# Moving some fifty entries of a hand-written step schedule in a decoder layer with three attention stages and a mixture of experts

## Chip, cores and metric
One core of a Trainium2 chip (trn2) runs the whole program in one launch. The metric is the device time of that core in microseconds (us). TensorE is called PE here, VectorE DVE, ScalarE ACT, GpSimd POOL, and SyncE, which issues nearly all DMAs, SP.

## The reference, cut to what matters
Sixteen sequences of 128 tokens with 256 channels go through three sublayers, each followed by a plain layernorm.

```
x = layernorm(x + attn(x))                 # stage A: 16 heads of 16, rope, causal
x = layernorm(x + xattn(x, mask, ctx))     # stage B: 32 heads of 8, rope, mask; and 32 adapter heads over ctx
x = layernorm(x + ffn(x))                  # ffn: stage C, 16 heads of 128; stage D, 4 experts, top 2
def attn(x):   q, k, v = split(x @ Wqkv.T + b); q, k = rope(q), rope(k)
               return softmax(q @ k.T * scale + causal) @ v @ Wo.T + bo
```

## The kernel before
**Steps and units.** Stages A and B are one long software pipeline over numbered steps, from -20 up. Each engine's program is a Python loop over the same step numbers: at every step it looks in dictionaries for what is due and emits it, so each engine has its work in an order fixed at build time. Engines meet at semaphores alone. A *unit* is four heads of one sequence. Stage A has 64 units, one in a step (steps 0 to 63), four for a sequence; stage B has 256 units, two in every even step from 64 on, sixteen for a sequence (eight of self-keys, with the mask, and eight of adapter keys).

**One unit.** `pass1` computes the scores with queries down the partitions (L541 or L547 put the mask in, L554 the products), and DVE takes the negated row maxima (L737). Once a sequence has all its maxima, `shift_parts` splits them into three bf16 parts (L450 to L456, four small operations, on DVE in A and on POOL in B), PE turns them (`shift`, L565) and SP writes them as rows into the stacked queries. `pass2`, 12 steps later in A and 28 in B, computes the scores with keys down the partitions, already shifted (L589); ACT takes the exponential (L985), in stage B after DVE has added the mask (`mask2` L746, then L978). `pv`, two steps later, multiplies by the values (L611). Maxima of unit n free the score bank of unit n + 2, so `pass1` is never more than two units ahead of DVE.

**Outputs of a sequence g.** `ends`: ACT copies the result out of its bank (L995, L997). `tos`: PE turns it (L621), and DVE divides in the next step (L757 to L777). `backs`: PE turns it back (L631), and ACT and DVE split it in the next step (L1007, `out_low` L788 and L791). `wos`: PE's output projection (six matmuls L472 to L474), and in the next step DVE's `residual` (L801, then the three layernorm statistics L695, L697, L699). Two steps after that POOL computes the power, and DVE's `finish` (L710; POOL in B) writes X at three.

**Inputs of a pair of sequences c.** `xts`: four transposes of x or of the context (L489), which ACT and DVE split at the next step (`x_high` L888, `x_low` L723). In the steps up to 64 DVE does `x_low` before its maxima. `projs`: projections of q and k (12 matmuls on PE; from pair 9 on in two halves, one step apart), from which `evacs` (ACT L907, L909), `ropes`, `sums`, `splits` (POOL and a few on DVE: L403, L416, L427, L437, L440; ACT L926, L929), `parts` (DMA out) and `stacked` (DMAs into the stack, three for a sequence and kind in A, six in B) follow at fixed distances. `vals`: value projections (six matmuls). `masked`, `clamps`: the mask. POOL clears and fills the value buffers of stage B at the steps of `INITS` (`init_values`, L1075), and ACT's `values` waits for that.

**Banks.** The small products of PE (transposes, projections, values, shifts, outputs) take three PSUM banks in turn, two from step 86 on. The table `home` gives the banks out in the order in which the dictionaries name the products, so a product waits until the one three (or two) before it in this order has been read.

**Within a step** PE does pass1, pass2, pv, then the small products in the order `xts`, second halves, `projs`, `masked`, `vals`, turns (`turned`, `tos`, `backs`), `wos`; from step `TURNED_FIRST` on the turns come first. DVE does `x_low`, maxima, the outputs (divide, `out_low`, residual), `shift_parts`, mask, rope, splits, clamp, finish; in the steps of `CHANGE` the outputs come before the maxima.

**The way into stage C.** From step 302 on the same loops also do the loads of stage C's first weights (`LOAD_W`, `LOAD_W2`, `LOAD_TABS`), the first layernorm (`NORMS`), the splits (`HIGHS` on ACT L1736, `LOWS` L1645, `X_LOW` L1507) and the first four projections (`PROJECTIONS`, six matmuls of 512 columns, L1518 to L1520) with their ropes (`ROPES`, DVE L1658, L1661, POOL L1822). Stages C and D have schedules of their own.

## Time and profile before

| | us |
|---|---|
| median of 3 runs (1191.92 to 1195.79) | 1195.52 |
| the profiled execution | 1195.52 |
| its span, first to last instruction | 1193.7 |
| stages A and B with their start-up, to the last unit's maxima | 527.2 |
| stages C and D, from 575 us | 618.7 |
| PE busy over the span | 1128.8 |
| DVE busy over the span | 993.6 |
| mean granted clock of PE | 0.990 |

The profiled execution took 1.8 us more than its span and lies on the median, so sums are made against 1195.5. Busy PE is not PE at its peak, as ends of matmuls are modelled; what counts in the schedule is where an engine sits idle, and for whom.

### The profile page before, as it was taken

What the parts mean: (1) busy time and instruction counts of PE and PEld (TensorE: products, weight loads), DVE (VectorE), ACT (ScalarE), POOL (GpSimd) and SP (SyncE); (2) the same over time, 40 slices, a digit from 0 to 9 for tenths busy, and PEclk for the clock granted to TensorE, in tenths of its full rate; (3) what the DMA queues carried; (4) which work ended last, traced back from release to release, by engine and by line L of the source; (5) the groups of instructions that cost most, each with busy time, mean ns of one, the idle gap of its engine ahead of it and who ended that gap; (6) DMA issues with size and microseconds to landing.
All of it is one profiled execution on the core that took longest, in us unless ns stands there. A gap on an engine that the chain in (4) does not pass through costs nothing.

```text
span 1193.7 us, 29551 instructions
## 1 busy us (share of the span) xinstructions
PE 1128.8 (95%) x11172; PEld 934.4 (78%) x11172; DVE 993.6 (83%) x2284; ACT 660.4 (55%) x1687; POOL 656.9 (55%) x706
## 2 busy tenths in 40 slices
PE   5899999899999999879999999999999999999997
PEld 5667666666776766546899899998999899997887
DVE  6768887888889898978888888888888888877977
ACT  5466554566766667565555444444444444558663
POOL 4467655545455455254778544544554454847665
PEclk9899999999999999999999999999999999999999
DMA  6875443334333433212222000000000100101111
GB/s 161 205 186 135 122 125 87 87 95 116 88 106 101 106 97 97 76 58 76 68 63 63 1 1 2 1 1 2 1 1 1 37 1 1 37 18 37 36 36 36
DMA packets 98670, 76.68 MB, mean 64 GB/s; under 512 B 73547, under 2 KB 86987, under 8 KB 98529
## 3 DMA queue, kind: packets, MB, share of 16 engines
q1 hardware_dynamic: 98529, 74.80, 23.1%
q8 instruction: 89, 1.46, 0.5%
q14 instruction: 52, 0.43, 0.1%
HBM read 53.86 MB, written 19.92 MB: 62 GB/s over the span
## 4 chain that ended last, share of the span: by engine, by line
PE 58%; DVE 23%; issue 7%; ACT 5%; POOL 3%; SPq 2%; DMA 2%; DVEq 0%; POOLq 0%; ACTq 0%
PE bank L1518 5%; DVE B_nr L737 4%; PE bank L1519 4%; PE bank L1520 4%; PE bank L1574 4%; PE bank L1547 4%; PE bank L611 4%; DVE PT L746 3%; PE bank L472 2%; PE bank L554 2%; SPq L1154 2%; PE bank L1534 2%; PE bank L1589 2%; PE bank L1587 2%; PE bank L1588 2%
## 5 line engine op out<-in xcount | busy, mean ns | idle before, releaser
L1822 POOL TENSOR_TENSOR C_QK<-C_t1b,C_t2b 128x512 f32<-128x512 f32 x128 | 168.9, 1320 | 226.6 <-DVE C_t2b L1661 226.0
L1658 DVE SCALAR_TENSOR_TENSOR C_t1b<-bank,C_bcol,C_tabs 64x512 f32<-64x512 f32 x256 | 192.0, 750 | 37.3 <-PE bank L1520 33.2
L737 DVE TENSOR_REDUCE B_nr<-bank 128x4 f32<-128x512 f32 x256 | 164.4, 684 | 22.6 <-PE bank L554 21.0
L1518 PE MATMUL bank<-C_XTh,C_Wh 128*128 128x512 f32 x256 | 111.9, 437 | 4.4 <-DVE C_t2b L1661 1.9
L985 ACT ACTIVATE PT<-bank 128x512 f32<-128x512 f32 x160 | 92.2, 598 | 39.8 <-PE bank L589 39.3
L1754 ACT ACTIVATE C_P<-bank,C_nm 128x128 f32<-128x128 f32 x256 | 90.7, 367 | 34.0 <-DVE C_nm L1671 32.4
L978 ACT ACTIVATE PT<-PT 128x512 f32<-128x512 f32 x96 | 59.3, 630 | 88.7 <-DVE PT L746 88.7
L1773 ACT ACTIVATE C_V<-bank 128x512 f32<-128x512 f32 x64 | 38.1, 597 | 124.1 <-PE bank L1536 122.5
L611 PE MATMUL bank<-PT,vpool 128*32 128x128 f32 x2048 | 97.4, 285 | 4.3 <-ACT PT L978 3.1
L1519 PE MATMUL bank<-C_XTl,C_Wh 128*128 128x512 f32 x256 | 101.2, 395 | 0.0
L1520 PE MATMUL bank<-C_XTh,C_Wl 128*128 128x512 f32 x256 | 100.8, 394 | 0.0
L1661 DVE SCALAR_TENSOR_TENSOR C_t2b<-bank,C_bcol,C_tabs 128x512 f32<-128x512 f32 x128 | 96.1, 751 | 1.8
L554 PEld LDWEIGHTS bank<-stk 48*128 48x128 bf16 (+1 forms) x1280 | 50.9, 96 | 52.3 <-issue 27.5
L554 PE MATMUL bank<-stk 48*128 48x128 bf16 (+1 forms) x1280 | 77.7, 221 | 9.6 <-DVE B_nr L737 8.9
L589 PE MATMUL bank<-stk 54*128 54x128 bf16 (+1 forms) x1280 | 76.5, 219 | 10.0 <-DVE PT L746 3.8
L1762 ACT ACTIVATE C_OTh<-bank,C_bcol 128x512 fp32r<-128x512 f32 x64 | 44.1, 690 | 73.6 <-PE bank L1574 73.0
L1682 DVE SCALAR_TENSOR_TENSOR C_OTl<-bank,C_bcol,C_OTh 128x512 fp32r<-128x512 f32 x64 | 47.9, 748 | 38.9 <-ACT C_OTh L1762 38.8
L705 POOL TENSOR_TENSOR rstd<-ve,mhalf 128x1 f32<-128x1 f32 x48 | 28.1, 584 | 91.1 <-DVE ve L699 91.1
L589 PEld LDWEIGHTS bank<-stk 54*128 54x128 bf16 (+1 forms) x1280 | 53.5, 95 | 27.8 <-DVE PT L746 6.8
L1534 PE MATMUL bank<-C_Wh,C_XTh 128*128 128x256 f32 x256 | 72.5, 283 | 1.6 <-DVE C_t2b L1661 1.3
L1587 PE MATMUL bank<-C_Wh,C_OTh 128*128 128x256 f32 x256 | 72.0, 281 | 0.4 <-DVE C_OTl L1682 0.4
L1535 PE MATMUL bank<-C_Wl,C_XTh 128*128 128x256 f32 x256 | 71.9, 281 | 0.0
(267 smaller groups left out, 3683.5 us busy)
## 6 DMA issues: line engine op xcount, KB each, us to landing
Adrq<-PB SPq DMA_DIRECT2D x16, 192.0 KB, 3.2
Adrk<-PB SPq DMA_DIRECT2D x16, 192.0 KB, 3.4
stk<-Adrq SPq DMA_DIRECT2D x16, 192.0 KB
stk<-Adrk SPq DMA_DIRECT2D x16, 192.0 KB
Bdrq<-PB SPq DMA_DIRECT2D x16, 192.0 KB, 2.7
stk<-Bdrq SPq DMA_DIRECT2D x32, 96.0 KB
Bdrk<-PB SPq DMA_DIRECT2D x16, 192.0 KB, 2.7
stk<-Bdrk SPq DMA_DIRECT2D x32, 96.0 KB
```

What stands on the lines that cost most here:

```text
L554: m = e.matmul(bank[n % 2][:, j * 128:j * 128 + 128], QS[L][i3][rows, h, :], (AS if kd else KS[L])[i3][rows, h, :], start=bool(kd), stop=b ...
L589: m = e.matmul(bank2(n)[:, j * 128:j * 128 + 128], (AS if kd else KS[L])[i3][rows, h, :], QS[L][i3][rows, h, :], start=bool(L), stop=bool( ...
L611: m = e.matmul(o[32 * j:32 * j + 32, c3 * 128:c3 * 128 + 128], vp[:, h, :], pt_of(n)[:, j * 128:j * 128 + 128], start=first or not L, stop ...
L737: e.tensor_reduce(dst, bank[n % 2][:, :].rearrange("p (a b) -> p a b", a=4), AX.X, ALU.max, negate=True).then_inc(sem("m_dve"), 1)
L1518: e.matmul(o[:, :], CWh[hp][:, cs], XCh[0][:, t, :], start=t == 0, stop=False)
L1519: e.matmul(o[:, :], CWh[hp][:, cs], XCl[0][:, t, :], start=False, stop=False)
L1520: m = e.matmul(o[:, :], CWl[hp][:, cs], XCh[0][:, t, :], start=False, stop=t == 1)
L1534: e.matmul(ob, XCh[0][:, t, xs], CWh[hp][:, cs], start=t == 0, stop=False)
L1587: e.matmul(o, OCh[:, bs], CWh[hp][:, cs], start=r == 0 and b % 2 == 0, stop=False, skip_group_check=True)
L1658: e.scalar_tensor_tensor(out=v4(t1b[kq][lo:lo + 64, :]), in0=v4(o[hi:hi + 64, :]), scalar=bc[hi:hi + 64, :], in1=tabsC[hi:hi + 64, 2 * kq ...
L1661: e.scalar_tensor_tensor(out=v4(t2b[kq][:, :]), in0=v4(o[:, :]), scalar=bc, in1=tabsC[:, 2 * kq, :].unsqueeze(1).to_broadcast([128, 4, 128 ...
L1822: e.tensor_tensor(QK[v % 3][:, kq, :], t1b[kq][:, :], t2b[kq][:, :], ALU.add).then_inc(sem("rc_pool"), 1)
```

## The change
Only numbers of the schedule change: no operation is added, removed or reshaped, and the same instructions run on the same engines in another order. `s` is the step number.

```diff
-    LOAD_B, SPLIT_B = (14, 20, 27, 26), (20, 27)
+    LOAD_B, SPLIT_B = (12, 20, 24, 28), (20, 27)
...
-    xts = places((-1,), (-2, -4), (-2, 4), (-8, 8))
-    projs = places((2, 6), (2, 6, 10), (0, 10, 13), (-4, 10, 13))
-    masked = places((), (11,), (23,), (18,))
-    clamps = {s - (6 if c < 10 else 7): c for s, (c, _) in masked.items()}
-    vals = places((3, 5), (0, 14, 8, 16), (19, 22, 20, 25), (6, 22, 26, 30))
+    xts = places((-1,), (-2, -4), (-2, 2), (-8, 8))
+    projs = places((2, 6), (2, 6, 10), (0, 8, 13), (-5, 10, 13))
+    masked = places((), (12,), (21,), (18,))
+    clamps = {s - (3 if c < 10 else 7): c for s, (c, _) in masked.items()}
+    vals = places((3, 5), (4, 15, 8, 16), (19, 22, 20, 24), (7, 23, 26, 30))
...
-        xts[bg0(c_) - (4 if c_ < 2 else 7)] = (c_, 0)
+        xts[bg0(c_) - (4 if c_ == 1 else 4 if c_ == 2 else 4)] = (c_, 0)
...
-        for b_, late in enumerate((0, (8, 7, 13)[ti_]) if c_ > 8 else (0, 0)):
+        for b_, late in enumerate((0, (7, 7, 13)[ti_]) if c_ > 8 else (0, 0)):
...
-        return end_step(g, kd) + (7 if 17 <= g < 31 and kd else 1)
+        return end_step(g, kd) + (7 if 16 <= g < 31 and kd else 1)
...
-        return to_step(g, 1) + (6 if g < 14 else 6 if g < 15 else 5 if g < 17 else 8 if g < 31 else 5)
+        return to_step(g, 1) + (4 if g < 14 else 4 if g < 15 else 8 if g < 16 else 8 if g < 31 else 5)
...
-    backs = {wo_step(g) - (2 if g == 14 else 4 if g == 15 else 3 if 16 <= g < 31 else 2): g for g in range(32)}
+    backs = {wo_step(g) - (2 if g == 14 else 3 if g == 15 else 3 if 16 <= g < 31 else 2): g for g in range(32)}
-    turned = {shift_step(g) + (2 if g < 17 else 4 if g < 31 else 2): g for g in range(32)}
+    turned = {shift_step(g) + (2 if g < 16 else 4 if g < 31 else 2): g for g in range(32)}
...
-    LOAD_W, LOAD_W2, LOAD_TABS, TURN, X_LOW, VALUES, LOAD_PAIR2 = 305, 330, 315, 319, 324, 352, 352
-    NORMS = [303, 304, 306, 307, 310, 312, 313, 314]
+    LOAD_W, LOAD_W2, LOAD_TABS, TURN, X_LOW, VALUES, LOAD_PAIR2 = 302, 332, 317, 319, 321, 352, 352
+    NORMS = [303, 305, 307, 309, 311, 312, 313, 314]
-    HIGHS, LOWS = [308, 310, 342, 351], [322, 323, 351, 352]
-    PROJECTIONS = {(0, 0): 326, (0, 1): 335, (1, 0): 341, (1, 1): 344}
-    ROPES = {(0, 0): 328, (0, 1): 339, (1, 0): 342, (1, 1): 345}
+    HIGHS, LOWS = [308, 310, 337, 351], [322, 323, 351, 352]
+    PROJECTIONS = {(0, 0): 327, (0, 1): 335, (1, 0): 341, (1, 1): 343}
+    ROPES = {(0, 0): 328, (0, 1): 338, (1, 0): 342, (1, 1): 344}
-    MASK_FIRST = 316
+    MASK_FIRST = 320
...
-    CHANGE = range(70, 82)
-    TURNED_FIRST = 87
+    CHANGE = range(66, 84)
+    TURNED_FIRST = 82
...
-    INITS = {28: (0, 0), 35: (0, 1), 53: (1, 0), 61: (1, 1), 67: (2, 0), 73: (2, 1), 80: (3, 0), 89: (3, 1)}
+    INITS = {31: (0, 0), 35: (0, 1), 55: (1, 0), 59: (1, 1), 63: (2, 0), 71: (2, 1), 79: (3, 0), 88: (3, 1)}
```

Written out, the main moves are these:

| what | step before | step after |
|---|---|---|
| stage A, x of pairs 2 to 7 turned (`xts`) | 8c - 27 | 8c - 24 |
| stage A, turned back, sequences 0 to 14 | 4g + 23 | 4g + 21 |
| stage A, output projection, sequences 0 to 14 | 4g + 25 | 4g + 23 |
| the same two, sequence 15 | 80, 84 | 84, 87 |
| POOL's filling of the fourth value buffer | 61 | 59 |
| first and second values of pair 8 on the self side | 44, 58 | 48, 59 |
| pair 9: context turned, keys projected, last stacks | 68, 74, 87 and 94 | 66, 72, 85 and 92 |
| sequence 16: to, back, output projection | 110, 112, 115 | 116, 121, 124 |
| stage B, q projection of pairs 10 to 15, halves | r = 28, 29 | r = 27, 28 |
| the second q stack of these pairs | r = 49 | r = 47 |
| the first two values of these pairs | r = 6, 22 | r = 7, 23 |
| stage C's last early projection | 344 | 343 |

Here r is the step less 64, modulo 32 (a pair of sequences of stage B takes 32 steps; 49 and 47 are those of the next period).

## Rows read from the trace of the kernel before

**Rows 1.** The page's first part: busy time of PE and DVE over the span.

```profile
PE 1128.8 (95%) x11172; PEld 934.4 (78%) x11172; DVE 993.6 (83%) x2284; ACT 660.4 (55%) x1687; POOL 656.9 (55%) x706
```

**Rows 2.** Windows, stretches: length, busy PE, PEld, DVE, ACT, POOL, PEclk, DMA, GB/s.

```profile
0.00:57.20 57.20, 40.78 (x311) 33.99 (x311) 40.80 (x68) 27.99 (x59) 28.56 (x36) 0.94 0.73 182
...
99.90:118.70 18.80, 18.80 (x208) 13.94 (x206) 16.00 (x36) 11.54 (x28) 13.53 (x20) 1.00 0.51 119
...
177.20:222.70 45.50, 41.88 (x451) 30.04 (x451) 36.23 (x88) 22.13 (x64) 25.23 (x46) 0.99 0.32 87
...
401.20:444.30 43.10, 41.76 (x652) 30.09 (x646) 38.52 (x76) 29.51 (x77) 22.45 (x30) 1.00 0.38 101
```

**Rows 3.** Timeline of DVE, steps 36 to 39 of stage A: start, length, instruction [idle before].

```profile
109.26 0.69 DVE L737 TENSOR_REDUCE A_nr<-bank 128x4 f32<-128x512 f32 x1 [1.14 <-PE bank L554]
...
110.49 0.60 DVE L788 SCALAR_TENSOR_TENSOR OTl<-bank,A_bcol,OTh 128x128 fp32r<-128x128 f32 x2
111.00 1.02 DVE L450 CAST A_nmb<-A_nr 128x16 bf16<-128x16 f32 x1
112.06 0.65 DVE L452 TENSOR_TENSOR A_nb<-A_nr,A_nmb 128x16 f32<-128x16 f32 x1
...
114.13 0.41 DVE L710 TENSOR_SCALAR X<-z,mv,rstd 128x256 f32<-128x256 f32 x1
114.45 1.28 DVE L737 TENSOR_REDUCE A_nr<-bank 128x4 f32<-128x512 f32 x2
...
116.85 0.68 DVE L737 TENSOR_REDUCE A_nr<-bank 128x4 f32<-128x512 f32 x1
```

**Rows 4.** Timeline of POOL in the same steps.

```profile
110.82 1.17 POOL L440 TENSOR_TENSOR PB<-y,PB 128x512 bf16<-128x512 f32 x1 [0.27 <-ACT PB L929]
111.95 1.42 POOL L416 TENSOR_TENSOR tt<-ab,vpool 128x256 f32<-128x256 f32 x2
```

**Rows 5.** Timeline of PE and DVE, step 34, with a projection of pair 6.

```profile
104.70 0.39 PE L472 MATMUL bank<-XTh,A_Wh 128*128 128x256 f32 x1
...
106.49 0.39 PE L541 MATMUL bank<-identb,causalTb 128*128 128x512 bf16 x1
...
105.04 1.28 DVE L737 TENSOR_REDUCE A_nr<-bank 128x4 f32<-128x512 f32 x2
```

**Rows 6.** Timeline of DVE and POOL, step 30: the residual beside a POOL operation.

```profile
97.00 0.43 DVE L695 BATCH_NORM_STATS2 stat<-z 128x6 f32<-128x256 f32 x1
...
96.72 1.16 POOL L437 TENSOR_TENSOR y<-y,PB 128x512 f32<-128x512 f32 x1 [0.74 <-ACT PB L926]
```

**Rows 7.** Timeline of PE: its waits at steps 16, 30, 62 and 92.

```profile
60.12 0.40 PE L589 MATMUL bank<-stk 99*128 99x128 bf16 x4 [2.85 <-DMA stk<-A_nmT]
...
96.18 0.22 PE L565 MATMUL bank<-identb,A_nmb 128*48 128x128 bf16 x1 [0.53 <-DVE XTl L723]
...
172.54 0.43 PE L611 MATMUL bank<-PT,vpool 128*32 128x128 f32 x8 [1.05 <-ACT OTf L995]
...
222.11 0.61 PE L554 MATMUL bank<-stk 48*128 48x128 bf16 x8 [1.45 <-DVE B_nr L737]
```

**Rows 8.** Timeline of PE and DVE in one period of stage B, steps 218 to 224.

```profile
394.26 0.40 PE L554 MATMUL bank<-stk 48*128 48x128 bf16 x8
...
394.03 0.41 DVE L791 TENSOR_TENSOR OTl<-bank,OTh 128x256 fp32r<-128x256 f32 x1
394.67 1.29 DVE L737 TENSOR_REDUCE B_nr<-bank 128x4 f32<-128x512 f32 x2 [0.23 <-PE bank L554]
...
401.19 1.29 DVE L737 TENSOR_REDUCE B_nr<-bank 128x4 f32<-128x512 f32 x2 [0.40 <-PE bank L554]
```

**Rows 9.** Timeline of PE, steps 344 and 348, on the way into stage C.

```profile
553.61 0.40 PE L589 MATMUL bank<-stk 54*128 54x128 bf16 x8
...
554.89 0.50 PE L1518 MATMUL bank<-C_XTh,C_Wh 128*128 128x512 f32 x1 [0.31 <-DVE C_t2b L1661]
...
559.26 0.39 PE L472 MATMUL bank<-B_Wh,OTh 128*128 128x256 f32 x1 [0.56 <-DVE OTl L791]
```

## The prediction
> **What bounds the kernel now.** I read the page's first part first, then the windows, then the timelines engine by engine. PE is busy for 1128.8 of 1193.7 us and DVE for 993.6 [rows 1]. The windows show where what is left lies. The start, to 57.2 us, holds 16.4 us of idle PE (57.20 - 40.78). In steps 32 to 39 of stage A PE is busy for all of 18.80 us and DVE for 16.00; a period of stage B takes 43.1 us with 41.76 of PE and 38.52 of DVE [rows 2]. So PE sets the pace in A and B, with DVE 10 to 15% behind, and the two are coupled tightly: maxima free score banks, and pass1 is at most two units ahead of them. No operation changes, so all that can change is PE's idle time, and an order can hurt as easily as help: in A some 15% of slack on DVE stands against PE's none.
>
> The start is bound elsewhere. PE waits 2.85 us at step 16 for a DMA of shift rows [rows 7]. That DMA stands behind SP's queue of stack DMAs, whose places the change doesn't move before it. What is gained before 60.1 us is therefore taken back at this wait, and stages C and D keep their own schedules.
>
> **Stage A, DVE.** Four steps make one group. DVE's run that matters starts with maxima(4k) and ends with maxima(4k+1), since pass1(4k+3) waits for the latter. Before, it holds divide, out_low (0.60), the four small operations, rope and finish (0.41), and lasts 5.8 us: from 109.26 to the first end in the row of 114.45 [rows 3]. The change puts the output projection two steps earlier, so out_low and finish leave the run for step 4k+2 and the residual enters it. Its four operations are all that DVE does from the end of the two maxima, 115.7, to the next at 116.85, so some 1.2 us [rows 3]. Taken plainly that is 1.2 - 0.6 - 0.4 = +0.2 us for the run.
>
> But the small operations aren't limited by themselves. L450 lasts 1.02 us and ends at 112.02, and POOL's L440 ends at 111.99; L452 takes 0.65 and ends with the first half of POOL's L416 [rows 3, 4]. They sit waiting for POOL. A start 0.6 us later (1.2 - 0.6) only shortens that wait, as 1.02 us of L450 has 0.8 us of it to give, and the run loses finish: -0.4 us. The residual's own operations keep their length beside POOL: L695 takes 0.43 us under a POOL operation of 1.16 [rows 6]. I take -0.4, and +0.6 (a run that gets longer by all that moves in ahead of the small operations, with finish's place not regained) stays as the upper end. The Trainium skill has the mechanism (SBUF — State Buffer, section "SBUF: two separate sides"): DVE and GpSimd lock a shared port pair, and the loser blocks for the whole instruction. By that rule the result is this -0.4; were the lengths the operations' own, it would be +0.2.
>
> PE's part of a group: the output projection (six matmuls, 0.70 us: L472 to L474 at 0.117 each) moves from step 4k+1 to 4k+3 and the turn back (0.22) the other way. That is -0.48 before pass1(4k+3) and +0.48 behind it. Where DVE's run ends first this sums to nothing; with the run at -0.4 it does so in nearly every group. Term: 0, upper end below.
>
> **Stage A, the x transposes.** In 8c - 24 a transpose stands at step 4k, and its x_low is the first thing DVE does in step 4k+1, right behind the long run. Giving out the banks in the new order, I find that the projection of step 4k+2 takes the bank of this transpose: step 26 behind that of pair 6, step 34 behind that of pair 7. At step 34 PE would start at 104.70; DVE's run ends at 105.04, less 0.4, plus x_low 0.68 is 105.3 [rows 5]. So PE waits 0.65 us there, and as much at step 26: +1.3. Against that goes the old conflict, 0.53 us at step 30, which waited for x_low of pair 7 [rows 7]: -0.5. Pair 5's transposes (0.41 us) move from step 13, where the wait at 60.1 covered them, to step 16: +0.4. At steps 40 to 43 both have the same two waits for x_low.
>
> **Other places up to step 96.** At step 62 PE waits 1.05 us for ACT's copy of the result; ACT stood in `values`, waiting for POOL to fill the value buffer at step 61 [rows 7]. It is filled at 59 now: -1.05. At step 92 PE waits 1.45 us for maxima, with nothing else due [rows 7]; the first half of pair 10's q projection (0.70 us) now fills this: -0.7. The moves of sequence 15, of pair 9 and of g = 16 shift work inside a stretch with 3.6 us of idle PE (45.50 - 41.88) [rows 2]: 0, and 1.5 either way. `MASK_FIRST` changes nothing: the only output projection from 316 to 319 is at 316, and its residual's step 317 has no mask operation.
>
> **Stage B, six periods.** Before, steps 220 and 221 hold 18 matmuls (both halves of the q projection and the output projection) beneath 3.8 us of DVE work. The first half goes to step 219. PE's pass1(220), at 394.26, then starts 0.7 later, and DVE, free at 394.44, waits 0.93 instead of 0.23 [rows 8]. DVE gets 0.40 back at 401.19, where it waited for PE [rows 8]: +0.3 is left. The splits of q come one step earlier on POOL, so that POOL's sum of the two results can be earlier in step 230, where PE and DVE are both a little idle; that may give the 0.3 back. I take +0.1 a period, six times: +0.6. The bounds are -0.3 (all of that comes, and no delay) and +0.7 (nothing is absorbed): -1.8 and +4.2.
>
> **Way into C.** The last early projection (six matmuls of 512 columns, 1.4 us) goes ahead of pass2 at 344. It waits for L1661, before and after, and can't start ahead of 554.89; the 1.28 us of pass2 and pv from 553.61 to 554.89, which covered the wait, now come behind it: +1.28 [rows 9]. Later PE waits 0.56 for out_low at 559.26, which absorbs as much [rows 9]: +0.7 is left. HIGHS at 337 puts 1.06 us of ACT where exponentials are due, X_LOW goes ahead of LOWS on POOL, the norms lie in odd steps: +0.1 together, bounds -1 and +1.
>
> **Sum.** 1.3 - 0.5 + 0.4 - 1.05 - 0.7 + 0.6 + 0.7 + 0.1 = +0.85 us: 1195.5 + 0.8 = 1196.3.
>
> **Rivals.** 0.3% is 3.6 us, about what a measurement of this kernel can tell from no change.
>
> *No measurable change* is the forecast, 0.42.
>
> *Slower, DVE's run in A.* Place: step 4k, where the residual now stands ahead of the small operations. If these move away from POOL's operations instead of ending with them, or POOL is late too, the run grows by 0.6 instead of shrinking by 0.4. Seven of the groups of steps 24 to 60 then have DVE last (those without an x transpose or a moved value projection): 7 x 0.6 = 4.2, and both x_low waits grow by 1.0: +2.0. With the 0.8 of the sum this makes +7.0: 1202.5. It passes 0.3% from about 0.1 us a group on, with the two waits. For it: DVE's slack in A is only 15% [rows 2], and even at step 34, where PE has work to spare, pass1(35) at 106.49 comes 0.8 us after the first maxima of the row of 105.04 [rows 5]. Against: L450's length [rows 3, 4]. Chance 0.16.
>
> *Slower, stage B.* The 0.7 us isn't absorbed: +4.2 instead of +0.6, 1199.9. For it: between its waits at 394.67 and 401.19 DVE has 6.1 us of work on end [rows 8]. Against: 0.40 of idle DVE right behind. Chance 0.14.
>
> *Faster.* The new order spreads PE's small products: in stage B 6, 12 and 12 matmuls where 6 and 18 stood, in A none beside the long run. With the waits of 0.53, 1.05 and 1.45 gone (-3.0), x_low in time (0), stage B at -1.8 and the way into C even, it is about -4.8: 1190.7. For it: 3.6 us of idle PE from 177 to 223 and 1.3 in each period [rows 2]; against: each such gap is behind one particular operation. [...] Chance 0.28.
>
> **How the numbers follow.** Predicted is the likeliest case, 1196.3. With it, its own range is 1192 to 1199. The range takes in the faster case to 1190 and most of the slower ones to 1203. Faster 0.28, same 0.42, slower 0.30 (0.16 + 0.14).
>
> **What would show it.** In the profile after: PE waiting about 0.65 us for L723 at the projections of steps 26 and 34; no waits of 0.53 at step 30 and 1.05 at step 62; L450 shorter than 1 us in A, and L454 still ending with L416; step 16's wait at about 60 us still there; the periods of stage B at 43.1 to 43.4 us; L589 of the pair 316 behind the projection. The prediction is wrong if a period of B changes by more than 0.5, if the 120 us from step 16 to 64 change by more than 3, or if a stretch of half granted clock comes or goes with a new or a lost wait (the windows show 0.94 in the start [rows 2]).

## The result, and the profile after

| | before | after |
|---|---|---|
| median, us | 1194.85 (1191.92 to 1195.79, 6 runs) | 1205.91 (1202.71 to 1207.78, 6 runs) |
| the profiled execution, its span | 1195.52, 1193.7 | 1203.91, 1202.1 |
| granted clock over the span | 0.990 | 0.988 |

The ratio is 1.0094 (95% interval 1.0079 to 1.0109): the change costs 11 us, 0.94%. The forecast was 1196.3, and its range ended at 1203.

The page's first part answers to [rows 1]: PE is busy for 4.0 us more, DVE for 3.6 less, with the same instructions. No work came in; what was lost is order, and in this profile a little clock.

```profile
PE 1132.8 (94%) x11172; PEld 934.2 (78%) x11172; DVE 990.0 (82%) x2284; ACT 659.2 (55%) x1687; POOL 654.7 (54%) x706
```

**A trap ahead.** The two profiles can't be laid side by side as they are. At the first maxima of step 64 the kernel before stands at 177.16 and the one after at 176.88, which looks like a stage A that cost nothing. But the profiled execution of before had a stretch of half granted clock at 61.7 us, right behind the wait of step 16, and the one after had none there. The experiment with the new way into C alone (below, `tail_alone`) has the order of the kernel before up to step 302 and a clock like that after: both show two stretches of half clock ahead of step 16 and none from there to step 64. So it is the ruler for everything ahead of step 318. "Ruler" below always means this run. Windows, columns as in [rows 2]: first the kernel before from step 16 to 20, then `tail_alone`, cut at the first maxima of steps 16, 20, 64, 152, 284 and 318.

```profile
57.16:71.42 14.26, 11.41 (x114) 7.81 (x114) 5.11 (x10) 7.88 (x16) 5.91 (x7) 0.88 0.74 200
```

```profile
57.42:68.64 11.22, 9.90 (x114) 6.88 (x114) 5.11 (x10) 8.03 (x17) 6.19 (x7) 1.00 0.90 229
68.64:174.33 105.69, 102.14 (x1109) 74.74 (x1108) 89.36 (x196) 64.80 (x161) 69.26 (x101) 1.00 0.54 136
174.33:301.00 126.67, 119.84 (x1643) 85.23 (x1645) 105.73 (x219) 76.24 (x199) 65.12 (x99) 0.99 0.37 97
301.00:477.31 176.31, 170.28 (x2656) 122.88 (x2646) 157.03 (x307) 120.67 (x313) 90.49 (x117) 1.00 0.37 99
477.31:522.15 44.84, 37.72 (x645) 24.32 (x639) 41.78 (x89) 25.32 (x54) 12.99 (x19) 1.00 0.29 81
```

The kernel after, cut at the same maxima:

```profile
56.76:69.03 12.27, 10.39 (x118) 7.34 (x118) 5.72 (x11) 8.72 (x18) 6.26 (x7) 1.00 0.72 185
69.03:176.88 107.85, 103.42 (x1115) 75.33 (x1114) 88.36 (x200) 64.11 (x161) 67.67 (x100) 1.00 0.55 136
176.88:304.20 127.32, 118.94 (x1638) 83.42 (x1641) 104.76 (x217) 76.00 (x199) 66.01 (x100) 1.00 0.36 96
304.20:484.62 180.42, 171.83 (x2656) 122.60 (x2644) 157.06 (x306) 120.64 (x312) 90.50 (x117) 1.00 0.36 97
484.62:530.00 45.38, 37.78 (x645) 24.37 (x639) 41.79 (x90) 25.34 (x54) 12.98 (x19) 1.00 0.29 81
```

The same order takes 14.26 us with a clock of 0.88 and 11.22 with 1.00. Not all of these 3.04 us is the clock: PE's busy time differs by 1.51 (11.41 against 9.90), and the rest is the wait of step 16 for its DMA, 2.85 us before and 1.32 in the ruler. In the eleven kernels that have the order of before up to this wait it took from 0.44 to 2.85 us. Without it steps 16 to 20 take 9.90 or 9.91 us in the five of them with full clock there.

Against the ruler the change costs 1.05 us in steps 16 to 20, 2.16 to step 64, 0.65 to step 152, 4.11 to step 284 and 0.54 to step 318; 0.66 us of it had been won before step 16 (57.42 - 56.76). That is 7.85 us; the way into C brings the rest. Of the 1.05 us, 0.56 is a longer DMA wait (1.88 against 1.32) and 0.49 the order (10.39 against 9.90). The ruler's third window holds a stretch of half clock that the kernel after doesn't have, so the 0.65 us there are too few; against `q_half_alone`, which has none either, they are 1.23.

**Stage A.** PE's waits after (timeline of PE; the last is on the way into C):

```profile
58.75 0.40 PE L589 MATMUL bank<-stk 99*128 99x128 bf16 x4 [1.88 <-DMA stk<-A_nmT]
83.43 0.39 PE L472 MATMUL bank<-XTh,A_Wh 128*128 128x256 f32 x1 [0.72 <-DVE XTl L723]
103.97 0.39 PE L472 MATMUL bank<-XTh,A_Wh 128*128 128x256 f32 x1 [0.72 <-DVE XTl L723]
220.16 0.38 PE L472 MATMUL bank<-B_Wh,XTh 128*128 128x256 f32 x1 [1.12 <-DVE z L801]
555.98 0.64 PE L611 MATMUL bank<-PT,vpool 128*32 128x128 f32 x8 [0.71 <-ACT PT L978]
```

The waits for x_low at steps 26 and 34 are there, at 0.72 each (forecast 0.65); those of 0.53 and 1.05 of [rows 7] are gone. The wait at 220.16 is new. DVE and POOL at step 36, timelines, answer to [rows 3, 4]:

```profile
109.05 0.69 DVE L737 TENSOR_REDUCE A_nr<-bank 128x4 f32<-128x512 f32 x1 [0.80 <-PE bank L554]
...
111.49 0.32 DVE L450 CAST A_nmb<-A_nr 128x16 bf16<-128x16 f32 x1
...
112.52 0.66 DVE L454 CAST A_nmb<-A_nb 128x16 bf16<-128x16 f32 x1
...
113.90 1.29 DVE L737 TENSOR_REDUCE A_nr<-bank 128x4 f32<-128x512 f32 x2
```

```profile
110.61 1.16 POOL L440 TENSOR_TENSOR PB<-y,PB 128x512 bf16<-128x512 f32 x1 [2.10 <-ACT PB L929]
111.73 1.42 POOL L416 TENSOR_TENSOR tt<-ab,vpool 128x256 f32<-128x256 f32 x2
```

L450 shrank from 1.02 to 0.32 us and still ends with L440 (111.81 and 111.77); L454 ends with L416 (113.18 and 113.15). From the first maxima to the next it is 4.85 us (113.90 - 109.05) where it was 5.19 (114.45 - 109.26): the run of DVE got 0.34 shorter, and -0.4 was forecast. Here the trace agrees with the rule of the Trainium skill that the prediction cited (SBUF — State Buffer, section "SBUF: two separate sides").

**Stage B.** Steps 218 to 224 after, timelines of PE and DVE; they answer to [rows 8]:

```profile
396.36 0.39 PE L472 MATMUL bank<-XTh,B_Wh 128*128 128x256 f32 x1 [0.37 <-DVE OTl L791]
...
397.27 0.40 PE L554 MATMUL bank<-stk 48*128 48x128 bf16 x8
```

```profile
395.89 0.42 DVE L791 TENSOR_TENSOR OTl<-bank,OTh 128x256 fp32r<-128x256 f32 x1
397.71 1.29 DVE L737 TENSOR_REDUCE B_nr<-bank 128x4 f32<-128x512 f32 x2 [1.40 <-PE bank L554]
...
404.17 1.29 DVE L737 TENSOR_REDUCE B_nr<-bank 128x4 f32<-128x512 f32 x2 [0.36 <-PE bank L554]
```

The half projection (396.36) waits for out_low, which holds the bank that it takes, and out_low stands behind the maxima on DVE. Then come its six matmuls, then pass1, then DVE, which has been idle for 1.40 us instead of 0.23.

And the 0.40 us at 401.19, which was to give part of it back, is still 0.36. PE was on its way to give it back: it starts pass1 of step 222 at 400.02, 1.32 us ahead of DVE's maxima (401.34), where it had been 0.59 ahead. But then its value product waits for ACT's copy out of the projection's bank (L907). This copy stands on ACT behind an exponential (L978) that waits for DVE's mask operation, which follows the late maxima. Timelines of PE and ACT after:

```profile
401.83 0.39 PE L472 MATMUL bank<-B_Wh,XTh 128*128 128x256 f32 x1 [0.50 <-ACT ab L907]
```

```profile
399.62 1.23 ACT L978 ACTIVATE PT<-PT 128x512 f32<-128x512 f32 x2 [2.96 <-DVE PT L746]
...
401.13 0.65 ACT L907 ACTIVATE ab<-bank 128x256 f32<-128x256 f32 x2
```

All four profiles with pairs 12 to 15's half at the new step have this wait of 0.50 us in each of the four periods, and none of the other fourteen has it. (This is read from the traces; no run takes this wait away alone.)

DVE's idle 1.40 us stands at steps 156, 188 and 252 too. The maxima come 1.17 us later at each of the four places, and 0.15 comes back within the period.

### The profile page after: what moved, and what is told of

The parts are those of the page before. It is cut to its first block, busy times and chain, and to the rows that moved or that the text cites. A ratio compares the mean times of both kernels' runs of the same rounds, so it can differ in the third digit from the quotient of the medians.

```text
span 1202.1 us, 29553 instructions
## 1 busy us (share of the span) xinstructions
PE 1132.8 (94%) x11172; PEld 934.2 (78%) x11172; DVE 990.0 (82%) x2284; ACT 659.2 (55%) x1687; POOL 654.7 (54%) x706
## 3 DMA queue, kind: packets, MB, share of 16 engines
q8 instruction: 89, 1.46, 0.5%
## 4 chain that ended last, share of the span: by engine, by line
PE 61%; DVE 23%; issue 7%; ACT 5%; DMA 2%; POOL 2%; SPq 1%; DVEq 0%; POOLq 0%; ACTq 0%
PE bank L1518 5%; PE bank L1519 5%; PE bank L1520 4%; PE bank L1574 4%; PE bank L611 4%; PE bank L1547 4%; DVE B_nr L737 3%; PE bank L547 3%; DVE PT L746 3%; PE bank L472 3%; PE bank L554 2%; PE bank L589 2%; PE bank L1534 2%; PE bank L1589 2%; PE bank L1587 2%
## 5 line engine op out<-in xcount | busy, mean ns | idle before, releaser
L737 DVE TENSOR_REDUCE B_nr<-bank 128x4 f32<-128x512 f32 x256 | 164.5, 685 | 27.0 <-PE bank L554 25.9
L978 ACT ACTIVATE PT<-PT 128x512 f32<-128x512 f32 x96 | 59.4, 630 | 91.6 <-DVE PT L746 91.6
L440 POOL TENSOR_TENSOR PB<-y,PB 128x512 bf16<-128x512 f32 x36 | 42.2, 1171 | 54.9 <-ACT PB L929 54.6
```

The source lines that it names most:

```text
L737: e.tensor_reduce(dst, bank[n % 2][:, :].rearrange("p (a b) -> p a b", a=4), AX.X, ALU.max, negate=True).then_inc(sem("m_dve"), 1)
```

## The experiments

Each was timed in five rounds beside the kernel before; a ratio is to that kernel, with its 95% interval. 1% is 12 us. "Maxima" are the starts of L737 in the profile, against `tail_alone`, the ruler.

### The q projection's half, and who waits for whom

`q_half_alone`, on the kernel before:

```diff
-    projs = places((2, 6), (2, 6, 10), (0, 10, 13), (-4, 10, 13))
+    projs = places((2, 6), (2, 6, 10), (0, 10, 13), (-5, 10, 13))
```

> The kernel before with one number changed: the first half of stage B's q projection at r = 27 (-5 where it has -4). Theory 1: 1.17 us in each of the four periods from step 156 on and about as much in the two before, 5 to 7 us slower: 1200 to 1202 us. Theory 2: 0.6 us slower, 1195.5 us, and the periods stay at 43.1 us. A third possibility is that the half costs its full price only together with the values' move from r = 6 to 7: then this kernel shows 0.70 a period, 4.2 us, with no wait for out_low.

1198.25 us, ratio 1.0049 (1.0032 to 1.0065): this one number is half of the loss. The timeline of DVE at step 220:

```profile
394.29 1.29 DVE L737 TENSOR_REDUCE B_nr<-bank 128x4 f32<-128x512 f32 x2 [1.39 <-PE bank L554]
```

PE's half projection waits 0.38 us for out_low there, without the values' move, so the third possibility falls. From step 152 to 284 the maxima lose 4.13 us, four times 1.03. Pairs 10 and 11 lose nothing, against theory 1: no out_low stands ahead of their halves.

`q_half_back`, the changed kernel:

```diff
-    projs = places((2, 6), (2, 6, 10), (0, 8, 13), (-5, 10, 13))
+    projs = places((2, 6), (2, 6, 10), (0, 8, 13), (-4, 10, 13))
```

> The changed kernel with one number back: the first half of stage B's q projection at step r = 28 again (-4 where the change has -5). Theory 1: the half stands between maxima n and pass1 n + 2, in a loop of PE and DVE that has no slack: its six matmuls (0.70 us) and a wait of 0.37 us for out_low, whose bank it takes, push DVE's next maxima back by 1.17 us and nothing is given back later. Four periods show exactly 1.17 us, the two before them something near it: the kernel gets 4.7 to 7 us faster, 1199 to 1201 us, and DVE's idle 1.40 us in front of the maxima of steps 156, 188, 220 and 252 goes back to 0.2. Theory 2, the prediction's term: the half costs 0.1 us a period and the 1.17 us have another cause (the order of the banks, the values one step later): 0.6 us faster, 1205.3 us, and the idle time stays.

1200.01 us, ratio 1.0054 (1.0038 to 1.0070): 0.40% less than the change (1.0094 - 1.0054), 4.8 us. DVE's idle time at step 220 is 0.24 again. Theory 1's price holds from both sides; its split into wait and matmuls does not, as the next run shows.

`back_early`, the changed kernel with the turn back a step earlier:

```diff
-    backs = {wo_step(g) - (... else 3 if 16 <= g < 31 else 2): g for g in range(32)}
+    backs = {wo_step(g) - (... else 4 if 16 <= g < 31 else 2): g for g in range(32)}
```

> The changed kernel with the turns back of stage B's sequences one step earlier (four steps ahead of the output projection instead of three), so that out_low stands behind the maxima one unit earlier and the q projection's first half finds its bank read. Theory: of the 1.17 us a period that the half costs, 0.37 us is the wait for out_low and goes; the 0.70 to 0.8 us of matmuls stay: four periods, 1.5 us faster than the changed kernel, and the idle time of DVE before the maxima of steps 156, 188, 220 and 252 goes from 1.40 to 1.0 us. Rival: out_low, 0.42 us, ahead of the maxima of the unit before takes the place of the wait: no gain, and a wait of PE for maxima instead. A third: the bank rule makes something else late, and it is slower.

1200.70 us, ratio 1.0052 (1.0037 to 1.0066), 5.0 us less than the change where 1.5 had been expected (in the profiles it is 3.1 between steps 152 and 284). DVE at steps 154 and 156:

```profile
306.15 0.42 DVE L791 TENSOR_TENSOR OTl<-bank,OTh 128x256 fp32r<-128x256 f32 x1
...
309.51 1.29 DVE L737 TENSOR_REDUCE B_nr<-bank 128x4 f32<-128x512 f32 x2 [0.87 <-PE bank L554]
```

out_low now stands ahead of the maxima (307.36), and the half doesn't wait. A period costs 0.26 us instead of 1.03 (the maxima stand 3.89 us behind `tail_alone`'s at step 152 and 4.91 at step 284, four periods later). My split of the 1.17 us into 0.37 of wait and 0.70 of matmuls was wrong. Without the wait most of the 0.70 us lies beside the maxima on DVE, for which pass1 waits anyway; with it, the whole half starts only when DVE has done the maxima and out_low, and nothing hides it. The bank's wait was worth some 0.8 us a period.

`b_back_only` is the control: the same diff on the kernel before.

> The kernel before with the turns back of stage B's sequences one step earlier (four steps ahead of the output projection) and the q projection's halves where they were. In the changed kernel this move was worth 0.8 us a period. Theory: it was worth that because the first half waited for out_low's bank; with the half at r = 28 nobody waits for it at r = 27, and the move gives nothing or costs a little, as out_low (0.42 us) now stands ahead of the maxima of r = 26: 0 to +0.3 us in each period, 0 to 1.5 us slower. Rival: the move helps by itself, 0.8 us in each of four or five periods: 3 to 4 us faster, 1190 us, and the best version.

1196.99 us, ratio 1.0028 (1.0015 to 1.0042). The move alone gains nothing: it costs 0.24 us a period, and 1.7 us about step 112, where sequence 16's turn back moves. So it was worth its 0.8 us only for the half.

### The way into stage C, and the clock

`tail_alone`: the new LOAD_*, X_LOW, NORMS, HIGHS, PROJECTIONS and ROPES on the kernel before; `tail_back`: the old ones on the changed kernel.

> The kernel before with the change's numbers for the way into stage C alone (loads, NORMS, HIGHS, LOWS, X_LOW, PROJECTIONS, ROPES). In the two profiles this stretch cost 3.9 us more after the change. Theory 1: some 2.7 us of it are a stretch of half granted clock that went on for 10.2 us where 3.4 had been, which hangs on the moment at which the chip looks and not on this order; the order itself costs 0.7 us (exponentials behind the split of HIGHS) and 0.4 us (the last projection ahead of pass2): 1.0 us slower in the median, 1195.9 us. Theory 2: the order causes the longer stretch of half clock: 3 to 4 us slower, 1198 to 1199 us, with 0.60 or less of granted clock in the profile's windows from 530 to 540 us.

> The changed kernel with the numbers of the way into stage C as before. Theory 1 (the long stretch of half clock isn't this order's doing): 1.0 us faster than the changed kernel, 1204.9 us. Theory 2 (it is): 3 to 4 us faster, 1202 to 1203 us, and the stretch of half clock near 540 us is 3.4 us long.

1194.84 us, ratio 1.0013 (1.0003 to 1.0023), and 1202.88 us, ratio 1.0085 (1.0071 to 1.0098), 0.09% less than the change: 1.1 to 1.6 us, theory 1. The 1.1 us of `tail_back` lie inside the intervals (the change's starts at 1.0079); the 1.6 us of `tail_alone` are clear of the kernel before (its interval starts at 1.0003). Yet the clock in the profiles went with the order. Windows of 20 us from the last maxima on, of before, after, `tail_alone` and `tail_back`:

```profile
528.00:548.00 20.00, 16.57 (x260) 9.97 (x260) 13.23 (x28) 15.27 (x29) 11.94 (x12) 0.91 0.21 70
```

```profile
532.00:552.00 20.00, 17.01 (x212) 10.27 (x212) 12.23 (x24) 13.04 (x25) 11.10 (x13) 0.74 0.12 35
```

```profile
524.00:544.00 20.00, 16.85 (x212) 10.32 (x212) 12.19 (x25) 12.96 (x25) 11.07 (x13) 0.74 0.13 33
```

```profile
535.00:555.00 20.00, 16.83 (x264) 10.00 (x266) 13.29 (x28) 15.29 (x29) 11.77 (x12) 0.91 0.23 70
```

Both with the new order have 0.74, both with the old one 0.91. But `back_early`, with the new order, had one short stretch of half clock there (3.4 us), and `q_half_alone`, with the old one, a longer one (6.8 us). Over all profiles, a stretch of 10.2 us came in two of the four with the new order and in none of the fourteen with the old one, where the longest was 6.8. Whether the order makes the long stretch likelier stays open; the medians bound what it costs.

### Stage A

`x_alone`, on the kernel before:

```diff
-        xts[bg0(c_) - (4 if c_ < 2 else 7)] = (c_, 0)
+        xts[bg0(c_) - (4 if c_ < 2 else 4)] = (c_, 0)
```

> The kernel before with the x transposes of pairs 2 to 7 at 8c - 24 instead of 8c - 27, and nothing else. The prediction's own steps give two new waits of 0.65 us for x_low at steps 26 and 34, and the old wait of 0.53 at step 30 gone: +0.8 us, 0.07% slower. Between kernels with the same clock history the profiles of the old and the new order of stage A differ by 2.2 us from step 20 to step 64. Theory 1: the transposes cost more than their waits, as 0.66 us of them and x_low ahead of the maxima now stand in steps 4k and 4k + 1, where PE or DVE has nothing to spare: 1.8 to 2.5 us from step 20 to 64, 0.2% slower. Theory 2: the outputs' move carries the rest: 0.8 us here. In times alone the two are within the uncertainty; the maxima's starts in the profile tell them apart.

1195.56 us, ratio 1.0014 (1.0005 to 1.0023). From step 20 to 64 the maxima lose 0.39 us, nearer to the prediction's 0.8 than to theory 1. Its steps 16 to 20 had a stretch of half clock at 59.6 us. Less the DMA wait they take 11.91 us, and 11.41 in `out_alone`, which has the old order there and a like stretch at 59.9: pair 5's transposes cost 0.5 us, where +0.4 was forecast. The kernel after shows the same price at full clock (10.39 against 9.90).

`out_alone`, on the kernel before:

```diff
-        return to_step(g, 1) + (6 if g < 14 else 6 if g < 15 else 5 if g < 17 else 8 if g < 31 else 5)
+        return to_step(g, 1) + (4 if g < 14 else 4 if g < 15 else 5 if g < 17 else 8 if g < 31 else 5)
```

> The kernel before with the output projections of sequences 0 to 14, and the turns back two steps ahead of them, two steps earlier, and nothing else. The prediction has 0 for it (PE's -0.48 and +0.48 cancel, DVE's run is 0.4 us shorter), and as a rival +0.6 us in each of seven groups, 4.2 us. Theory 1: the run is shorter (L450 goes from 1.02 to 0.32 us), but PE, with the projection's 0.70 us now behind pass1 of 4k + 3, delays the maxima of 4k + 4 by 0.7 us where the run gives back 0.3 to 0.5: +0.1 to +0.2 us a group, +1.3 us from step 20 to 64, 0.1% slower. Rival 1: the prediction's 0 holds, and the profile shows less than 0.3 us from step 20 to 64. Rival 2: +4.2 us, 0.35% slower.

1197.65 us, ratio 1.0033 (1.0020 to 1.0046), 3.9 us, and 2.9 us of maxima from step 20 to 60 (2.0 at steps 61 and 62, where DVE has given its share back). The prediction had 0. The view of PE's waits from 70 to 168 us (waiting operation, releaser, sum, times, longest):

```profile
PE bank L565 <- DVE XTl L723: 0.9, 2, 0.6
PE bank L621 <- DVE XTl L723: 0.9, 1, 0.9
PE bank L472 <- ACT ab L909: 0.8, 1, 0.8
PE bank L489 <- DVE XTl L723: 0.7, 1, 0.7
PE bank L621 <- DVE OTl L788: 0.6, 1, 0.6
PE bank L541 <- DVE A_nr L737: 0.3, 2, 0.2
```

They sum to 4.2 us; in `tail_alone` from 68.6 to 164 us they sum to 2.5 (0.9, 0.6, 0.5, 0.3, 0.2), and none is for L737 or L788. Some 1.7 us more are thus waits, most of them of small products for a bank. The rest is seen at steps 38 to 40, the timeline of PE in `out_alone`:

```profile
115.41 0.39 PE L541 MATMUL bank<-identb,causalTb 128*128 128x512 bf16 x1 [0.16 <-DVE A_nr L737]
...
118.95 0.39 PE L541 MATMUL bank<-identb,causalTb 128*128 128x512 bf16 x1
```

At 115.41 PE is early, since the output projection has left, and waits for maxima: what it saved isn't collected. At 118.95 the projection's 0.70 us stand in front, and maxima(40) come 0.78 us later against `tail_alone`, of which the shorter run gives 0.34 back. (From step 60 to 64 this profile loses 2.0 us more, beside a stretch of half clock at 175.9 us, so the timed 3.9 us are not all the order's.)

`a_back_only`, on the kernel before:

```diff
-    backs = {wo_step(g) - (2 if g == 14 ...
+    backs = {wo_step(g) - (4 if g < 14 else 2 if g == 14 ...
```

> The kernel before with the turns back of stage A's sequences 0 to 13 two steps earlier (step 4g + 21), their output projections left at 4g + 25. Stage A's outputs moved together cost 2.9 us from step 20 to 60 in the profile. Theory: that price is the output projection's, whose 0.70 us now stands ahead of pass1 of 4k + 4 and is missed by nobody ahead of pass1 of 4k + 3, which waits for maxima; the turn back is 0.22 us and out_low leaves a run that ends with POOL anyway: less than 0.5 us either way from step 20 to 60, no change in the times (within 0.1%). Rival: the turns back and out_low carry the price or a gain of their own: 0.2 us a group, 2 us.

1202.16 us, ratio 1.0073 (1.0055 to 1.0091). Theory and rival are both far off: a move of 0.22 us of matmuls costs 8.7 us. PE's waits from 73 to 176 us:

```profile
PE bank L472 <- DVE XTl L723: 3.3, 2, 1.8
PE bank L565 <- DVE OTl L788: 2.6, 3, 1.6
```

Both are new. With the turn back two steps earlier, `home` gives the shift (L565) a bank that out_low still has to read, and PE, which works in its order, stands still. The larger sum is two projections, at steps 30 and 41, that now wait for x_low (1.51 and 1.80 us). Two stretches of half clock inside stage A (at 128.7 and 156.0 us) came with it in the profile, so the 8.7 us are waits and clock together.

### The stretch from step 60 to 128

`init_g16`: the new INITS, and sequence 16 at the places of the later ones (`to_step` + 7, `wo_step` + 8, `turned` + 4), on the kernel before.

> The kernel before with two parts of the change that the profiles show as gains: the filling of the value buffers at the new steps (INITS, the fourth at step 59) and sequence 16's output at the places that the later sequences have (to_step + 7, then 8, turned + 4). Theory: the wait of 1.0 us at step 62 goes, and about 0.5 us around steps 112 to 128: 1.0 to 1.5 us faster than before, 0.1%, and the best version of all so far. Rival: each gain is given back at the next wait behind it (the maxima of step 64, the q stack of step 126): no change.

1194.11 us, ratio 0.9996 (0.9988 to 1.0005): the rival. Timeline of PE at step 64:

```profile
173.48 0.50 PE L547 MATMUL bank<-B_MKh,B_identr 128*128 128x512 f32 x1 [0.82 <-DMA stk<-Bdrk]
```

The wait of 1.0 us at step 62 is gone, and the first unit of stage B waits 0.82 us for its keys' DMA instead. Sequence 16 gives 0.9 us from step 110 to 130, but the maxima of step 96 come 2.0 us later; what that is, the last two runs tell.

`three_back`: the changed kernel with the half, stage A's outputs and the way into C as before.

> The changed kernel with three of its parts as before: the q projection's first half at r = 28, stage A's output projections and turns back at their old steps, and the numbers of the way into stage C. Theory: the prices are additive, and of the 0.94% that the change costs these three carry 0.40 + 0.33 + 0.09 to 0.13%: 0.1% above the kernel before is left, 1195.5 us. Rival: a part that was taken at nothing (the stretch from step 64 to 128, the values, the loads) costs on its own: 0.3% or more above before.

1196.30 us, ratio 1.0035 (1.0021 to 1.0048): the rival. 4.2 us are left, and the maxima lose 2.0 of them from step 64 to 128. So I looked at sequence 15, whose residual was waited for at 220.16.

`seq15_alone`, on the kernel before (projection at 87 instead of 84, turn back at 84 instead of 80):

```diff
-        return to_step(g, 1) + (... 5 if g < 17 ...)
+        return to_step(g, 1) + (... 8 if g < 16 else 5 if g < 17 ...)
-    backs = {wo_step(g) - (... 4 if g == 15 ...
+    backs = {wo_step(g) - (... 3 if g == 15 ...
```

> The kernel before with sequence 15's output projection at step 87 instead of 84 and its turn back at 84 instead of 80, as in the change, and nothing else. With three parts of the change undone 0.35% is still left, and in that profile 1.2 us come at one place: the value product of step 88 waits 1.12 us for the residual of sequence 15 (L801), whose bank it takes. Theory: this part alone costs about that, 0.8 to 1.5 us between steps 84 and 92, 0.1% slower. Rival: without the moves of pair 9 around it the product of step 89 meets the residual when it has long been done: no change, and the price of the stretch from 64 to 92 belongs to the parts together.

1195.52 us, ratio 1.0017 (1.0004 to 1.0029), and 1.0 us of maxima between steps 84 and 92. The wait is the very one: at 219.74 PE's L472 waits 1.12 us for L801.

`four_back`: as `three_back`, with sequence 15's output back too.

> The changed kernel with four parts as before: the three of the run before (the q projection's first half, stage A's outputs, the way into stage C) and sequence 15's output. Theory: 1.2 us less than with three, 0.25% above the kernel before, and no wait of 1.12 us for L801 at step 88. Rival: the wait only moves to another product, as the small products of these steps share two banks: still 0.35%.

1197.34 us, ratio 1.0035 (1.0023 to 1.0046): the rival again. The wait for L801 is gone and another stands near its place, for maxima:

```profile
224.34 0.40 PE L554 MATMUL bank<-stk 48*128 48x128 bf16 x8 [1.63 <-DVE B_nr L737]
```

The wait of 1.45 us at step 92 stands behind it as before. So these prices don't add: alone the part costs 1 us, and taken out of the whole it gives nothing back. What of the 4.2 us belongs to pair 9, the values and the loads wasn't tried.

### What was worth having

`half10`, on the kernel before, in a blank line behind the loop over `xts`:

```diff
+    projs[bg0(10) - 5] = projs.pop(bg0(10) - 4)
```

> The kernel before with the first half of the q projection one step earlier for pair 10 alone (step 91 instead of 92), not for pairs 11 to 15. Theory: at this one place the half fills a wait of 1.45 us for maxima and no other product has to be read first, and the profiles of kernels that have it show no half granted clock near 220 us where the others have 0.83 over 10 us: 0.8 us earlier maxima from step 96 on, up to 2 us with the clock, 0.1% faster. Rival: the 0.8 us are given back before step 112, or what looks like a gain is a clock that varies from one execution to the next: no change.

1192.36 us, ratio 0.9986 (0.9974 to 0.9998): 1.7 us faster than the kernel before, with an interval that just leaves out 1. At step 92, where PE waited 1.45 us [rows 7], 0.32 is left; the maxima come 0.8 us earlier than the ruler's at step 96 and still 0.6 at step 160.

But that gain isn't the filled wait. The ruler and the kernel before have a stretch of half clock at this place, and `half10` has none. `out_alone` has none either, and it keeps the half at step 92 and its wait (at 225.45, 1.46 us for L737). Windows from the maxima of step 88 to those of step 152, of `out_alone` and of `half10`:

```profile
222.18:306.58 84.40, 79.11 (x1222) 56.01 (x1225) 72.55 (x137) 55.63 (x142) 40.97 (x59) 1.00 0.39 104
```

```profile
216.72:301.13 84.41, 79.44 (x1222) 56.09 (x1225) 72.59 (x138) 55.50 (x141) 40.87 (x59) 1.00 0.39 103
```

At full clock both orders take the same time: moved into the wait, the half costs nothing and gains nothing, as pass1 waits there for DVE's maxima either way. The ruler takes 85.03 us over the same steps and the kernel before 85.49, both at a clock of 0.98. What `half10` gained in the profile is this clock. Its timed gain goes the same way: the mean granted clock of its twelve executions is 0.992, that of the 23 of before beside them 0.990. The expectation took the full clock near 220 us for a mark of the moved half; `out_alone` and `a_back_only`, which don't move it, have full clock there too.

`half10_g16` adds sequence 16's places to it.

> The same with sequence 16's output at the places of the later sequences, which showed 0.5 us of gain from step 112 to 128 in a profile. Theory: the two add up, 1.3 us in the profile and up to 2.5 us with the clock, 0.1 to 0.2% faster than before: the best version of the study. Rival: within 0.1% of the kernel before.

1195.66 us, ratio 1.0010 (0.9999 to 1.0021): neither the best nor faster. The 0.9 us from step 110 on are there, but PE waits at step 96, and the half clock is back at 226.5 us:

```profile
226.25 0.62 PE L547 MATMUL bank<-B_MKh,B_identr 128*128 128x512 f32 x1 [1.43 <-DMA stk<-Bdrk]
```

`half10_out16`: the same, but sequence 16's shift rows are turned at step 82 as before, not at 84.

> The kernel before with pair 10's half at step 91 and the outputs of sequence 16 (to_step + 7, output projection + 8) at the places of the later ones, but its shift rows turned at step 82 as before (turned + 2, not + 4). Theory: where the rows were turned two steps later, SP issued their four DMAs and the twelve stack DMAs behind them some 2 us later, and the keys of step 96 were waited for (1.43 and 1.60 us for stk<-Bdrk); with the turn at its old place that wait goes and the 0.9 us that the outputs give from step 110 to 130 stay: faster than the kernel with the half alone, 0.2% faster than before. Rival: the wait of step 96 has another cause (the outputs' banks), and this is at 0.1% above before again.

1192.80 us, ratio 0.9996 (0.9987 to 1.0005). The theory holds in the profile: the wait is gone, the maxima of step 96 come when `half10`'s do, and the 0.9 us stay. The view of SP's queue, first of `half10_g16`, then of `half10_out16`:

```profile
212.53 0.98 SPq L1154 DMA_DIRECT2D Bdrk<-PB  x2
213.55 3.05 SPq L1154 DMA_DIRECT2D stk<-B_nmT  x4
...
220.57 3.76 SPq L1154 DMA_DIRECT2D stk<-Bdrk  x6
```

```profile
211.76 2.22 SPq L1154 DMA_DIRECT2D stk<-B_nmT  x3
214.02 1.02 SPq L1154 DMA_DIRECT2D Bdrk<-PB  x2
...
219.01 3.76 SPq L1154 DMA_DIRECT2D stk<-Bdrk  x6
```

Turned two steps later, the rows of sequence 16 (stk<-B_nmT) stand in the middle of SP's queue and push the keys behind them back: 220.57 against 219.01, and 2.5 us against the step, whose maxima stand 0.9 us earlier in `half10_g16`. In time this version isn't told from `half10` or from the kernel before (its profile has a stretch of half clock at 60.4 us that `half10`'s hasn't). So `half10` is the one version timed as faster: by little, with one interval of sixteen that just leaves out 1, and not by its order at full clock.

## Why the prediction was wrong, step by step

In this table "measured" is the maxima's loss against `tail_alone`, or the timed ratio where named.

| step of the prediction | forecast | measured |
|---|---|---|
| x transposes, with the old wait gone | +0.8 | +0.4 alone (`x_alone`) |
| stage A's outputs, PE and DVE | 0 (rival 4.2) | +2.9 alone to step 60; timed +3.9 |
| values and the filling at step 62 | -1.05 | -0.9 after; 0 alone |
| pair 5 at step 16 | +0.4 | +0.5 (after, and `x_alone`) |
| first half in the wait of step 92 | -0.7 | 0.0 at full clock (`half10` beside `out_alone`) |
| sequence 15, pair 9, sequence 16 | 0, 1.5 either way | +1.0 for 15 alone; for 16 -0.9, and +2.4 by SP's queue |
| stage B | +0.6 (bounds -1.8, +4.2) | +4.1; timed +4.8 to +5.9 |
| way into C | +0.8 | timed +1.1 to +1.6 |

**Three steps failed, and the first two carry most of the loss.** The first is stage B: "DVE, free at 394.44, waits 0.93 instead of 0.23 [rows 8]. DVE gets 0.40 back at 401.19, where it waited for PE [rows 8]: +0.3 is left." Neither half of it holds: DVE waited 1.40 us, and got 0.04 back at the second place. The 0.40 us at 401.19 wasn't slack, since PE's lead was lost in its new wait of 0.50 us for ACT's L907, and ACT was late because DVE's maxima and mask were. And the 0.7 us wasn't the upper bound: the half's bank had to be read by out_low first, and it could not start beneath the maxima. I had given out the banks for the x transposes of stage A and not for this step. The rival for stage B, 0.7 us a period, had the place and not the price, 1.03 us in four of the six periods.

The second is stage A's outputs: "-0.48 before pass1(4k+3) and +0.48 behind it. Where DVE's run ends first this sums to nothing". The condition was the wrong way round. Where DVE's run ends last, PE's -0.48 only buys a wait for maxima (115.41), while the +0.70 behind it delays pass1(4k+4) in full. Beyond that the banks' order changed, with 1.7 us more of waits. The rival for stage A had nearly the right sum, +4.2, for the wrong reason: DVE's run did get shorter.

The third is "the first half of pair 10's q projection (0.70 us) now fills this: -0.7". It does fill the wait, and the time doesn't change (84.41 us beside 84.40). PE waits there for DVE, and matmuls placed within that wait didn't bring DVE's maxima forward. The maxima 0.8 us earlier that look like this forecast are the clock's, so that number came by luck.

**What held.** The waits for x_low at steps 26 and 34, in place and size; the run of DVE, which ended with POOL's operations as read; the wait at step 16, still there; pair 5's +0.4; `MASK_FIRST`, which moves no instruction of DVE (the order of its instructions from step 310 on is the same in `tail_back`, which has the new number, and in the kernel before). The way into C was 0.8 us against a measured 1.1 to 1.6: ACT's split of C_Wh (L1736) ahead of exponentials costs PE the 0.71 us of 555.98, a wait that `tail_alone` has too and the two profiles with the old order don't; the prediction had it within "+0.1 together, bounds -1 and +1".

Of the signs that the prediction named for being wrong, two came. A period of B grew by 1.03 us, where it allowed 0.5, and the half clock near 222 us went with the wait of step 92. Steps 16 to 64 took 120.12 us beside 120.00 and seemed unchanged; beside the ruler they took 3.21 more, of which 0.56 is the DMA wait and 2.65 the order.

The sum of the forecast's losses and gains (+0.85) rested on gains that are not kept: the filling of the value buffers was worth nothing alone, since a DMA was next in line; sequence 16's outputs were worth 0.9 us, and the turn that the change moved with them cost more on SP's queue, which the prediction did not follow at this place. The faster case, 0.28, was argued from idle time in the windows. Of the 1.3 us of idle PE in each period 1.1 is waiting for DVE's maxima and mask, and no order tried here collected it. The faster case's sum, -4.8, also takes 1.45 for a wait that the forecast prices at 0.7 and leaves out pair 5's +0.4. And the rival for stage A would pass 0.3% from 0.2 us a group on, not 0.1 (0.85 + 7 x 0.2 + 2 x 0.6 is 3.5).

**What stays open:** some 2 us in the steps 64 to 128 that no single part explains; whether the new way into C lengthens the half clock; and whether the half at step 91 makes the half clock near 222 us rarer.

## What to carry to other kernels

Before a small operation is moved, write out which buffer it then gets and which operation has to have read that buffer, and on which engine and behind what this reader stands; here a move of 0.70 us of matmuls cost 1.03 us a period, most of it for that reason, and one of 0.22 us cost 8.7 us in all, with the half clock that came with it.

Idle time between two engines that feed each other isn't slack by itself. Matmuls put into PE's wait of 1.45 us for maxima gained nothing at full clock, and the same matmuls put ahead of the pass1 that DVE waits for cost over their own length. Before counting on a later gap, follow what else stands between: here it was ACT's copy, late for the same reason.

And compare two profiles stretch by stretch at the same granted clock and with the same DMA waits. Here 1.5 us of clock and 1.5 us of a DMA's wait in the profile before hid that the new order took 3 us more, and 0.6 us of clock passed for a filled wait.

## What the runs showed of the hardware

The same 114 matmuls of steps 16 to 20 stand in 14.26 us at a mean granted clock of 0.88 (`before`) and in 11.22 at 1.00 (`tail_alone`), both from one order. Less the DMA wait in them (2.85 and 1.32 us) these are 11.41 and 9.90. Of the ten kernels that have this order and at most one short stretch of half clock (3.4 us), the five with one lie at 11.39 to 11.42 and the five without at 9.90 or 9.91: one such stretch, at 1.2 instead of 2.4 GHz, cost 1.5 us.

The wait of step 16 for its DMA took 0.44 to 2.85 us in eleven kernels whose order is the same up to there. A difference of two such profiles at this place is no effect of a change.

Nearly all stretches of half clock, over the eighteen profiles, lie at the same five places: in the start-up, behind the DMA wait of step 16, near 222 us behind the wait of 1.45 us, behind the last maxima of stage B, and in the last 5 us. All eighteen have one in the start-up, behind the last maxima and at the end; at step 16 ten have one. Near 222 us, of the eleven profiles with pair 10's half at step 92 nine had it. Of the seven with the half at step 91 six had full clock, and the seventh (`half10_g16`) was the one with a new wait of 1.43 us there. That a filled wait keeps the clock up is therefore likely, not shown. Where it came, steps 88 to 152 took 85.03 (`tail_alone`) and 85.49 us (`before`), and 84.40 where it didn't (`out_alone`).
